# The first block product placed ahead of the low-rank product in groups two to four of a four-layer kernel, and S2 split ahead of T3

## The reference

```
x = x + x @ w_eff.T                          # 0: weight quantized to 8 levels, plus a low-rank delta
x = x + x @ W1.T + 2 * gated low-rank term   # 1: logits = x @ Wr.T (+5 for the sequence's language),
                                             #    top 2 of 8 experts, softmax, ranks of 16
x = x + x @ W2.T + b + 2 * (x @ A[s]) @ B[s] # 2: one adapter of rank 16 per sequence, of 32
x = x + x @ W3[i].T                          # 3: one 1024 x 1024 weight per sequence, of 16
```

## Time and profile before

| | us |
|---|---|
| median of three runs | 638.99 |
| profiled execution | 638.79 |
| its span | 637.0 |
| TensorE busy | 631.9 (99%) |
| VectorE busy | 501.4 (79%) |
| ScalarE busy | 364.7 (57%) |
| GpSimd busy | 90.3 (14%) |

### The profile page before, as it was taken

One profiled execution on the slowest core, in us unless ns is written; L12 is line 12 of the kernel. 1 busy time (PEld: TensorE's weight loads), 2 busy tenths in 40 slices (PEclk: granted clock), 3 DMA queues, 4 the chain that ended last, 5 costly groups with the idle time before them and its releaser, 6 DMA issues.

```text
span 637.0 us, 10326 instructions
## 1 busy us (share of the span) xinstructions
PE 631.9 (99%) x3992; PEld 584.5 (92%) x3992; DVE 501.4 (79%) x645; ACT 364.7 (57%) x549; POOL 90.3 (14%) x120
## 2 busy tenths in 40 slices
PE   8999999999999999999999999999999999999997
PEld 8899999999999999999889999889999889999886
DVE  6899999879991538988887778888687989686753
ACT  6674583972731336745774746665655765664553
POOL 2210225003210010001220001231001223000120
PEclk9999999999999999999999999999999999999999
DMA  8772112111104001213673222684213485002372
GB/s 285 209 206 75 59 33 67 34 33 34 34 0 133 1 1 34 63 64 101 208 253 125 67 67 68 199 261 161 68 34 100 147 283 190 1 1 67 131 245 86
DMA packets 46020, 67.32 MB, mean 106 GB/s; under 512 B 3604, under 2 KB 32020, under 8 KB 45972
## 3 DMA queue, kind: packets, MB, share of 16 engines
q1 hardware_dynamic: 40900, 58.28, 29.0%
q10 hardware_dynamic: 5072, 8.39, 3.8%
HBM read 58.27 MB, written 8.39 MB: 105 GB/s over the span
## 4 chain that ended last, share of the span: by engine, by line
PE 99%; DVE 0%; POOL 0%; issue 0%; POOLq 0%
PE ps L1263 30%; PE ps L1261 30%; PE ps L1262 30%; PE ps L1406 4%; PE ps L1404 1%; PE ps L1272 1%; PE ps L1434 1%; PE ps L1357 1%; PE ps L1450 0%; PE ps L1462 0%; PE ps L1460 0%; PE ps L1442 0%; DVE tmp L1249 0%; DVE tmp L1251 0%; POOL ident L540 0%
## 5 line engine op out<-in xcount | busy, mean ns | idle before, releaser
L1263 PE MATMUL ps<-e_both,ring_lo 128*128 128x384 f32 (+3 forms) x384 | 133.3, 347 | 0.0
L1261 PE MATMUL ps<-e_both,ring_hi 128*128 128x384 f32 (+3 forms) x384 | 133.1, 347 | 0.0
L1262 PE MATMUL ps<-x_both,e_both 128*128 128x256 f32 x448 | 123.7, 276 | 0.0
L899 DVE TENSOR_TENSOR e_both<-raw,e_both 128x512 fp32r<-128x512 f32 x128 | 90.7, 733 | 28.1 <-ACT e_both L773 27.7
L1262 PE MATMUL ps<-e_both,e_mid 128*128 128x512 f32 (+2 forms) x288 | 109.2, 379 | 0.0
L1261 PE MATMUL ps<-e_both,e_mid 128*128 128x512 f32 (+2 forms) x288 | 109.1, 379 | 0.0
L1263 PE MATMUL ps<-e_both,e_mid 128*128 128x512 f32 (+2 forms) x288 | 109.1, 379 | 0.0
L773 ACT ACTIVATE e_both<-raw 128x512 fp32r<-128x512 f32 x128 | 78.8, 628 | 51.5 <-PE ps L1263 51.2
L589 POOL TENSOR_TENSOR raw<-raw,ident 128x128 f32<-128x128 f32 x64 | 47.3, 741 | 338.8 <-DMA raw<-w_t 338.8
L1262 PEld LDWEIGHTS ps<-x_both,e_both 128*128 128x128 f32 x448 | 84.1, 188 | 0.0
L1263 PEld LDWEIGHTS ps<-e_both,ring_lo 128*128 128x128 f32 x384 | 72.1, 188 | 5.5
(11 more groups left out here) (175 smaller groups left out, 1264.4 us busy)
## 6 DMA issues: line engine op xcount, KB each, us to landing
raw<-w_t SPq DMA_DIRECT2D x64, 512.0 KB, 4.1
w_w<-x_t SPq DMA_DIRECT2D x16, 512.0 KB, 3.8
w_w<-w SPq DMA_DIRECT2D x15, 512.0 KB, 5.3
y<-tmp ACTq DMA_DIRECT2D x30, 256.0 KB, 3.5
e_both_w<-w_t SPq DMA_DIRECT2D x5, 512.0 KB, 7.8
e_both_w<-w_t SPq DMA_DIRECT2D x4, 384.0 KB, 6.0
e_mid_w<-bs SPq DMA_DIRECT2D x24, 64.0 KB, 3.0
e_mid_w<-b_cat SPq DMA_DIRECT2D x4, 128.0 KB, 5.9
```

The costliest lines, as they stand in the source:

```text
L899: return dve.tensor_tensor(out, whole, hi.bitcast(F32), ALU.subtract)
L1261: pe.matmul(out, a[0], b_[0], start=start, stop=False, **kw)
L1262: pe.matmul(out, a[0], b_[1], start=False, stop=False, **kw)
L1263: return pe.matmul(out, a[1], b_[0], start=False, stop=stop, **kw)
```

## The change

On TensorE, from the second group on, product 0 is issued first and the low-rank product behind it; in the first group the order stays. On ScalarE, in all four groups, S2's split and the keep of product 0 stand ahead of the wait for `t_done`, the copy of the projections and T3's split. On VectorE, in all four groups, S2's low part stands ahead of T3's. On SP the load of the next group's B11 waits for `t_done` too, since the low-rank product, which reads B11's parts, is no longer ahead of product 0.

```diff
--- before.py
+++ after.py
@@ -486,7 +486,10 @@
                 elif op == "B12":
                     sp.wait_ge(t_done, g)
                 else:
+
                     sp.wait_ge(prod, NP * (g - 1) + {"B11": 1, "B22": 4, "B21": 6}[op])
+                    if op == "B11":
+                        sp.wait_ge(t_done, g)
                 k, j = divmod(i, 2)
                 sp.dma_start(x_whole[op], x[g:g + 1].rearrange("g p (k t) -> p (g k) t", t=TG)
                              [:, 4 * k:4 * k + 4, TB2 * j:TB2 * (j + 1)]).then_inc(s_x[op], 16)
@@ -806,12 +809,12 @@
 
             def group(g, last):
                 split_weight(g, "S1")
+                split_weight(g, "S2")
+                act.wait_ge(prod, NP * g + 1)
+                keep(0, x3_sum[0][0], 0)
                 act.wait_ge(t_done, g + 1)
                 act.activation(tok, ps[:, 4:8, TW:2 * TW], ACT.Copy).then_inc(part_done, 1)
                 split_x(g, "T3")
-                split_weight(g, "S2")
-                act.wait_ge(prod, NP * g + 1)
-                keep(0, x3_sum[0][0], 0)
                 act.wait_ge(s_bs, 96 * (g + 1))
                 for h in range(2):
                     act.activation(bs_half[h], bs_raw[:, h * 512:(h + 1) * 512], ACT.Copy).then_inc(bs_hi1, 1)
@@ -1503,12 +1506,15 @@
                             ins.then_inc(ring_free, 1)
 
             def group(g, last=False):
-                low_rank(g)
+
                 if g:
                     pe.wait_ge(y_free, 8 * (g - 1) + 4)
+                    block_product(g, 0, True)
+                    low_rank(g)
                 else:
+                    low_rank(g)
                     pe.wait_ge(chunk_out, 2 * N1 - 1)
-                block_product(g, 0, True)
+                    block_product(g, 0, True)
                 if g:
                     pe.wait_ge(y_free, 8 * g)
                 else:
```

## The result

The changed kernel takes 639.84 us (median of 20 runs, 639.42 to 640.46), the kernel before 639.03 us beside it (20 runs, 638.67 to 639.43). The ratio is 1.0013 with a 95% interval of 1.0007 to 1.0019: 0.8 us or 0.13% slower, within 0.2%, and yet not zero. The prediction had no change at 639.0 us and a range up to 640.1.

The account below looks back on a forecast made before the run. TensorE, busy 99% and never waiting after the start, was taken as the bound. Zero-cost terms gave 638.79 + 0 + 0 + 0 = 638.8 us, 639.0 in terms of the median; range 638.4 to 640.1.

Parts of the forecast that it names:

- the rival on S3: Group 0: S3's whole 1.3 us slip lands on TensorE, giving 640.3 us by the median; chance 0.02.
- TensorE's order: Groups two to four: block and low-rank products trade places, sum stays 13.54 us; cost 0, ends minus and plus 0.3 us.
- The cover taken from A11: First block product's operand, needed at y's end instead of 8.10 us later, still comes in time; cost 0.
- The low-rank product's end: Counter t_done comes at 351.07 instead of 345.63; ScalarE and VectorE work behind it still fits; cost 0.
- SP: Load of next group's B11 also waits on t_done; both counters come at 351.1 in either order; cost 0.
- group 0: First group: S3's low part 1.1 to 1.3 us later, spare 0.0 to 0.35 us; cost 0, ends 0 and 0.2.
- A11 was not late: Slower rival at y's end: a ScalarE or VectorE slip from 2.3 us on stalls TensorE; chance 0.03.
- a stall ahead of the low-rank product that goes: Faster rival: hidden wait for banks 6 and 7 after y vanishes; at most 0.1 us a group and seam; gain chance 0.02.

Follow-up runs that it names:

- the kernel with these edits alone: The kernel before with only the edits of ScalarE and VectorE, TensorE's order and SP's waits unchanged: 639.21 us, ratio 1.0000.

## Why the prediction was right, and which term was off

The mechanism was right: TensorE's own instructions set the time, none of them waits, and the operands all come in time. The time moved by less than the 0.2% that the prediction took as the limit of no change. One term of the sum was mis-sized, and it holds nearly all of the difference. A part is luck: 639.84 us lies beyond the 0 to 0.3 us that had 0.93 of the chances, and also beyond 639.39 + 0.3, the upper end without the 0.4 us of room for the rival on S3, which cost nothing. And with 20 runs on each side the interval leaves out no change, so that a difference under 0.2% could be told from none here.

- **TensorE's order** was put at 0, with ends of minus and plus 0.3 us for the seams. It measures +0.70 us. The seams are as predicted (0.23 us from y's last matmul to block 0). What failed is the sentence that the sum of 48 and 64 matmuls, 13.54 us, does not change: in the new place it is 13.76. The prediction looked at seams for an uncovered load and took a matmul's step as fixed by its shape. It named another pace of matmuls as one of two things that could alter the time, and then weighed it only as a gain, "more only if matmuls speed up, which no row shows". Its rows have one pace, but the trace of before has another too. In the preparation, behind 512-column matmuls, 72 matmuls of 256 columns from 39.48 us on step at 117.0 ns on average, and by line they are listed with up to 282 ns, not 276:

```profile
L1263 PE MATMUL ps<-e_both,ring_lo 128*128 128x256 f32 x16 | 4.5, 282 | 0.0
L1261 PE MATMUL ps<-e_both,ring_hi 128*128 128x256 f32 x16 | 4.5, 280 | 0.0
```

  In the last group's y, six 256-column matmuls between 512-column ones step at 118.8 ns. A grouping by line and shape, at these places of the trace, would have given an upper end that holds the 0.70: against 113.3 the steps are 3.7 and 5.5 ns longer, and 3 x 48 times that is 0.53 and 0.79 us.
- By the Trainium skill, "TensorE: Matmul & The Clock Gate", section "LDWEIGHTS (loading the stationary operand)", two uncovered loads a group would add some 0.6 us, the estimate in the prediction. That figure is near the 0.70 measured, but the trace does not show its mechanism: no seam has 0.1 us more than before, and the 0.21 us are spread over all 48 steps, 4.4 ns each on average. The Trainium skill, the same page, section "Back-to-back issue gap", gives N/2.4 + 2.5 ns as the gap of an isolated warm matmul of N columns, by which 256 columns would take 109.2 ns as an estimate. The trace, a stream of matmuls with a weight load each, has 113.3 and 117.8, two values for one shape.
- **The cover taken from A11**: right. The first low half ends at about 336.0, the second at 337.2; needed at 338.44 and about 341.3. Spare 2.4 and 4.1 us, predicted 2.3 and 3.7.
- **The low-rank product's end**: right. S2 was forecast for 343.3 to 345.3 and ran 344.35 to 346.36, less 0.91 that is 343.4 to 345.5; T3's high part, forecast to end at 353.0, ended at 354.0, less 0.91 that is 353.1.
- **SP** and **group 0**: right. SP's longer wait is late for nobody. S3 slipped by 1.1 us, the lower of the two forecasts, and the spare covered it: block 4 kept its 5.44 us, and the kernel with these edits alone is as fast as the one before.
- Of the rivals, A11 was not late, and S3's slip did not reach TensorE (no such wait in the view of TensorE's waits). The one on the faster side, a stall ahead of the low-rank product that goes, is excluded by the seam, which is 0.23 us long with either product behind y, a step of y itself.

What stays open is why one lead-in gives 113.3 and another 117.8 ns. Shown: it is not the copies of y's second half, their stores, the time behind y, the bank or the width alone; it changes with the tile that leads in; it lasts through the 48 matmuls of block 0, with every third weight load listed 4 ns longer, and the one cut that was tried ended it. Not shown: what in TensorE holds it; and whether it is the start column, the token block or only the rhythm of the low-rank tiles that tells them apart.

## What to carry to other kernels

Where one engine is busy all the time, the same instructions in another order need not add up to the same time: compare the step of one shape (the mean ns of a line, by form) at several places of the trace, and take the spread of these as the bound of the term. In this kernel 48 back-to-back matmuls took their pace from what stood ahead of them, so a change of order is to be checked on the stretch behind the seam, not only at the seam. At 0.1% the times of two kernels overlap, and the length of one block read from matmul starts, which repeats within 3 ns between groups, tells what the medians can't.

## What the runs showed of the hardware

- Back-to-back matmuls of 256 columns with a weight load each ran at two steady paces at the same granted clock of 1.00: 113.3 ns (listed 276 ns) and 117.8 ns (listed 281 ns).
- The slow pace lasted for all 48 matmuls of block 0 behind y, behind tile 0 and behind tile 1; one matmul cut in two ended it, with steps of 60, 109, 172 and 116 ns and then 113 to 114. At the slow pace one weight load in three was listed with 192 ns, at the fast one nearly all with 187 or 188.
- Matmuls with 96 rows in place of 128, among others of 128, cost more, not less: the 64 matmuls of a group's gates, 16 of them with 96 rows, step at 120.2 ns, and at 117.5 with all at 128.
